# One-hots by source in fp8, and block sums of masks and hops added by VectorE

## The chip, the cores and the metric

The kernel runs on one core of a Trainium2 chip. The metric is the device time of one execution in microseconds. TensorE (PE) multiplies matrices into PSUM, VectorE (DVE) and ScalarE (ACT) do elementwise work, GpSimd (POOL) issues the indirect DMAs, SyncE (SP) issues the plain ones.

## The reference

Four layers of a graph network run on 6250 nodes with 64 features and 200000 edges (`src`, `dst`, 32 edge features): a gated convolution with batch norm, a mean aggregation, three masked hops, and a message MLP. The change touches the first layer's preparation and the three hops. One hop is:

```
f1 = relu(x[src] @ nb_W + nb_b);  f2 = relu(x[dst] @ self_W + self_b)
h = relu(concat(f1, f2) @ att1_W + att1_b)
mask = clip(sigmoid(h @ att2_W + att2_b) * 1.5 - 0.45, 0, 1)
rowsum = segment_sum(mask, src) + 1e-6
d = clip(rowsum ** -0.5, 0, 10)
x = segment_sum((mask * d[src] * d[dst])[:, None] * x[dst], src);  out = out + x
```

## The kernel before, in words

Nodes lie in 49 blocks of 128 (node on the partition). Edges are sorted by source and, separately, by destination into 288 batches (`NBT`, `IT`) of 7 chunks (`BATCH`, `C`) of 128 edges; all edges of a batch belong to one block, and a table of block numbers (`m.table_s` by source, `m.table_d` by destination) lies in SBUF. A segment sum over a batch is 7 times a matmul of a 128x128 one-hot matrix (edge by node in the block) with the edges' values. For fp32 accuracy a value is split into three bf16 parts, so it takes 3 matmuls a chunk.

Stages run one after another, with barriers between them. Inside a stage each engine has its own instruction list, a loop over the iterations (`each12` unrolls twelve, `each4` four), and semaphores order the engines. The order inside each list is written by hand. Stages that the change touches:

- `stage_conv_spread` (L1099, once): per iteration it loads 126 KB of records, compares (VectorE, L1176) the record's node number with 0..127 into the one-hot by source, stores it to DRAM as `hot_s` (L1138, 224 KB in bf16), transposes it on TensorE (L1253) into `turned_s` (fp8, 112 KB), transposes the edge features into `e_turned` (L1141, 224 KB), multiplies, and scatters 452 KB of rows. ScalarE copies out of PSUM (L1213, L1219, L1220, L1231).
- `stage_masks` (L1895, three times): TensorE multiplies `turned_s` with the block's row part (L2014), ScalarE lays that down in one of 12 column buffers (L1968), a GpSimd indirect DMA adds the gathered column part to it (L1956), VectorE makes the logit (L2047, L2052), and for each four iterations (a quad) ScalarE takes the sigmoid (L1973) and VectorE's `weigh` (L2030) makes the masks and their three parts. TensorE's `collect` (L1995) sums a quad's masks, three quads later, into `sums`, one PSUM bank that holds 3 numbers for each of the 49 blocks. The block number comes from a register (`Blocks.of`, L119, reads four numbers of the table at once, L121). Zero matmuls (`add_zeros`) open and close the bank; at the end one copy moves it to `rowsum` (L2058).
- `stage_hop` (L2061, three times): GpSimd gathers 224 KB of rows (L2104), ScalarE weighs six chunks (L2120) and VectorE the seventh (L2134), VectorE takes off the upper bf16 parts (L2143, L2149), and TensorE multiplies with the one-hots (L2167) into `sums`, 49 blocks of 64 numbers over seven PSUM banks, at the block of a register. The end is again zero matmuls and one copy (L2153).
- The conv messages stage is not changed, but has the other form already: its `collect` on VectorE (L1608) adds a fixed PSUM place to a block of `acc` (L1615).

One-hots by source are loaded in `stage_masks` by quads (896 KB) and in `stage_hop` by iterations (224 KB), both on SyncE's queue, twelve iterations ahead. One-hots by destination (`hot_d`) stay in bf16.

Of the kernel before, what the change touches and what calls it, by code (L numbers as in the profile page):

```python
# [13 lines left out]
P = 128  # L14
# [1084 lines left out]
def stage_conv_spread(nc, m, src3):  # L1099
# [5 lines left out]
    with ctx:  # L1105
# [10 lines left out]
        onehot = sb("onehot", [P, 4, BATCH, P], bf16)  # L1116
# [13 lines left out]
        with nc.Block() as block:  # L1130
# [35 lines left out]
            def _(dve):  # L1166
# [4 lines left out]
                def prepare(it, i, k):  # L1171
                    dve.wait_ge(came[i], k * 16 + 16)
                    dve.wait_ge(hot_stored[i], k * 16 + 16)
                    dve.wait_ge(turn, it + 1)
                    dve.sem_inc(gate, 1)
                    nc.vector.tensor_tensor(onehot[:, i, :, :], b2(m.iota_p[:], BATCH), b3(rec[:, i, :, EF], P),  # L1176
                                            ALU.is_equal).then_inc(hot, 1)
                    e = rec[:, i, :, 0:EF]
                    rest, last = e4[:, i % 2, :, 1, :], e4[:, i % 2, :, 2, :]
                    nc.vector.tensor_tensor(rest, e, upper(e), ALU.subtract).then_inc(order, 1)  # L1180
                    dve.wait_ge(order, it + 1)
                    dve.sem_inc(gate, 1)
                    nc.vector.tensor_tensor(last, rest, upper(rest), ALU.subtract).then_inc(parted, 1)
# [711 lines left out]
def stage_masks(nc, m, l, row_part3, mask, rowsum):  # L1895
# [5 lines left out]
    with ctx:  # L1901
# [6 lines left out]
        onehot = sb("onehot", [P, 3, 4, BATCH, P], bf16)  # L1908
# [10 lines left out]
        sums = ctx.enter_context(nc.psum_tensor(f"{name}_sums_ps", [P, 512], fp32))[:, 0:3 * NB].rearrange("p (b c) -> p b c", c=3)  # L1919
# [5 lines left out]
        with nc.Block() as block:  # L1925
# [64 lines left out]
            @block.tensor  # L1990
            def _(pe):
                quads = Blocks(nc, pe, m.table_s)
                add_zeros(nc, m, sums, True)

                def collect(quad, s, k):  # L1995
                    pe.wait_ge(hot_came[s], k * 16 + 16)
                    pe.wait_ge(masked, quad + 1)
                    pe.sem_inc(gate, 1)
                    for h in range(4):
                        blocks = quads.of(quad * 4 + h, h)  # L2000
                        for t in range(BATCH):
                            last = nc.tensor.matmul(block_of(sums, blocks[0]), onehot[:, s, h, t, :], mask3[:, s, h * BATCH + t, :],  # L2002
                                                    start=False, stop=False)
                    last.then_inc(summed, 1)

                def step(it, s, i, k, more, _):
                    pe.wait_ge(staged, it + 1)
                    if i == 0:
                        pe.wait_ge(came[s], k * 16 + 16)
                    pe.wait_ge(laid, it + 1)  # L2010
                    pe.sem_inc(gate, 1)
                    for t in range(BATCH):
                        for n in range(3):
                            last = nc.tensor.matmul(part_ps[i][:, t, :], turned[:, s, i, t, :], now[:, i, n, :],  # L2014
                                                    start=n == 0, stop=n == 2)
                    last.then_inc(part, 1)
                    if i == 3 and (not isinstance(it, int) or it > 11):
                        collect(k * 3 + s - 3, s, k - 1)
                each12(pe, step, first=12)
                for s in range(3):  # L2020
                    collect(QUADS - 3 + s, s, KQ - 1)
                add_zeros(nc, m, sums, False).then_inc(summed, 1)

            @block.vector
            def _(dve):
                o = Order(dve, order)
                dve.sem_inc(hid, 12)
                dve.sem_inc(logits, 2)

# [12 lines left out]
                def step(it, s, i, k, more, order):  # L2042
# [10 lines left out]
                    if i == 3 and (not isinstance(it, int) or it > 3):  # L2053
                        weigh(k * 3 + s - 1, (s - 1) % 3, k, order)
                each12(dve, step, first=16, o=o, per=3 * 5)
                weigh(QUADS - 1, 2, KQ - 1, o)
                dve.wait_ge(summed, QUADS + 1)
                nc.vector.tensor_copy(rowsum, sums)  # L2058


def stage_hop(nc, m, name, mask, acc):  # L2061
# [4 lines left out]
    with ctx:  # L2066
# [5 lines left out]
        onehot = sb("onehot", [P, 3, 4, BATCH, P], bf16)  # L2072
# [3 lines left out]
        sums = ctx.enter_context(nc.psum_tensor(f"{name}_sums_ps", [P, 56, F], fp32))  # L2076
# [4 lines left out]
        with nc.Block() as block:  # L2081
# [47 lines left out]
            def _(dve):  # L2129
# [8 lines left out]
                def step(it, s, i, k, more, _):  # L2138
# [10 lines left out]
                    nc.vector.tensor_tensor(last, rest, upper(rest), ALU.subtract).then_inc(parted, 1)  # L2149
                scale_seventh(0, 0, 0)  # L2150
                each12(dve, step)
                dve.wait_ge(summed, IT + 5)
                nc.vector.tensor_copy(acc, sums[:, 0:NB, :])  # L2153

            @block.tensor
            def _(pe):
                blocks_s = Blocks(nc, pe, m.table_s)
                add_zeros(nc, m, sums[:], True)

                def step(it, s, i, k, more, _):  # L2160
                    pe.wait_ge(came[s * 4 + i], k * 16 + 16)
                    pe.wait_ge(parted, it + 1)
                    blocks = blocks_s.of(it, i)
                    pe.sem_inc(gate, 1)
                    for t in range(BATCH):
                        for q in range(3):
                            last = nc.tensor.matmul(block_of(sums, blocks[0]), onehot[:, s, i, t, :],  # L2167
                                                    upper(parts[:, i, q, t * F:(t + 1) * F]), start=False, stop=False)
                    last.then_inc(summed, 1)
                each12(pe, step)  # L2170
                add_zeros(nc, m, sums[:], False).then_inc(summed, 1)


def build(nc, a, out):
    m = Net()
    top = ExitStack()
    with top:
# [24 lines left out]
        m.hot_s, m.hot_d = (dram(n, [P, NBT, C * P // 2]) for n in ("hot_s", "hot_d"))  # L2202
# [215 lines left out]
```

## Time and profile before

| | |
|---|---|
| median of 3 runs | 12580.16 us (12571.6 to 12588.71) |
| profiled execution | 12564.72 us, span 12563.0 us |
| conv spread stage | 2459 to 3425 us of the span |
| masks stages | from 6870, 8550 and 10231 us, about 598 us each |
| hop stages | from 7757, 9438 and 11117 us, about 457 us each |
| busy share | PE 63%, PEld 59%, DVE 65%, ACT 55%, POOL 41% |
| DMA | 3241.49 MB, mean 258 GB/s |

Busy time is the time in which an engine executes operations; register, branch and semaphore instructions are not in it. PE is the matmuls, PEld the weight loads beside them. In a group's row the part behind the bar is how long the engine stood idle just before these operations, and what ended most of that. `DVEq` and the like are an engine's sequencer. A window's row gives the busy times in the order PE, PEld, DVE, ACT, POOL. Start times count from the span's start.

### The profile page before, as it was taken

To read this page: it belongs to the slowest core of one execution; us is meant where nothing else is said; L and a number is where in the kernel's file an instruction comes from. 1 tells how busy PE (TensorE), PEld (TensorE's weight loads), DVE (VectorE), ACT (ScalarE), POOL (GpSimd) and SP (SyncE) were. 2 spreads that over 40 slices of the span, in tenths; PEclk is the share of its full clock that TensorE was granted. 3 is DMA by queue.
4 is the path that set the end of the run, shared out by engine and by line. 5 is a ranking of instruction groups with operands and counts; after the bars stand their busy time and mean duration, and the time that the engine had idled before them with its cause. 6 is when DMAs were issued, how large, how long until landed. Compare 5 with 4: busy or idle time off the path is not lost. (4 is left out here: it accounts for less than half of the span.)

```text
span 12563.0 us, 438885 instructions
## 1 busy us (share of the span) xinstructions
PE 7912.2 (63%) x149095; PEld 7405.0 (59%) x149106; DVE 8207.7 (65%) x17786; ACT 6913.4 (55%) x17614; POOL 5175.5 (41%) x4482
## 2 busy tenths in 40 slices
PE   6444444488855549995766656666666666565765
PEld 6333333488745448885656656565665566565765
DVE  6777777588799999981750762925718527358047
ACT  1222222299855559986217448965479764587530
POOL 2777777444300001110630752706707338345044
PEclk8555555599978879998979669787697787787997
DMA  5555543299967759987949999979999799997997
GB/s 205 166 171 167 169 140 84 83 348 348 326 195 202 201 173 319 323 275 264 346 127 349 288 262 354 297 263 300 284 324 316 226 329 290 290 335 231 366 361 226
DMA packets 1430365, 3241.49 MB, mean 258 GB/s; under 512 B 392074, under 2 KB 973252, under 8 KB 1419042
## 3 DMA queue, kind: packets, MB, share of 16 engines
q1 hardware_dynamic: 1054798, 2289.98, 52.1%
q0 software_dynamic: 331264, 823.09, 24.7%
q10 hardware_dynamic: 44116, 125.96, 3.3%
q8 instruction: 113, 1.85, 0.1%
q14 instruction: 74, 0.61, 0.0%
HBM read 2042.53 MB, written 1129.76 MB: 253 GB/s over the span
## 5 line engine op out<-in xcount | busy, mean ns | idle before, releaser
L1956 POOL DMA_INDIRECT mask_cols<-cols_all,mask_index x864 | 1372.1, 1588 | 1339.1 <-ACT mask_index L1965 1172.0
L521 POOL DMA_INDIRECT rows_s<-place_rec,place_index x1568 | 1631.1, 1040 | 538.1 <-issue 528.7
L596 PE MATMUL place_slot_ps<-place_runs,place_oh_turned 50*128 50x100 f32 x3136 | 725.8, 423 | 1231.6 <-DVE place_runs L635 1213.6
L2104 POOL DMA_INDIRECT hop_x<-cols_all,hop_index x864 | 981.2, 1136 | 1237.4 <-ACT hop_index L2111 920.0
L596 PEld LDWEIGHTS place_slot_ps<-place_runs,place_oh_turned 50*128 50x128 f32 x3136 | 683.0, 327 | 1265.9 <-issue 1265.6
L2120 ACT ACTIVATE hop_parts<-hop_x,mask 128x64 f32<-128x64 f32 x5184 | 1265.4, 334 | 47.6 <-DMA hop_x<-cols_all,hop_index 28.1
L2047 DVE SCALAR_TENSOR_TENSOR mask_hidden<-mask_cols,att 128x448 f32<-128x448 f32 x864 | 538.5, 623 | 1085.5 <-DMA mask_cols<-cols_all,mask_index 1028.8
L2167 PE MATMUL hop_sums_ps<-hop_parts,hop_onehot 128*128 128x64 bf16 x18144 | 876.0, 216 | 472.3 <-DVE hop_parts L2149 398.2
L2167 PEld LDWEIGHTS hop_sums_ps<-hop_parts,hop_onehot 128*128 128x128 bf16 x18144 | 777.0, 113 | 573.6 <-issue 572.7
L1478 POOL DMA_DIRECT2D cm_onehot<-hot_d x288 | 152.1, 528 | 2031.1 <-POOLq L104 1229.9
L2014 PE MATMUL mask_part_ps<-mask_now,mask_turned 128*128 128x64 bf16 x18144 | 912.5, 231 | 37.4 <-issue 20.9
L1968 ACT COPY mask_cols<-mask_part_ps 128x448 f32<-128x448 f32 x864 | 460.5, 533 | 841.2 <-PE mask_part_ps L2014 829.9
L550 ACT COPY place_pair_now<-place_pair 128x8 f32 x196 | 38.7, 197 | 1599.0 <-issue 1585.6
L2014 PEld LDWEIGHTS mask_part_ps<-mask_now,mask_turned 128*128 128x128 fp8e4 x18144 | 888.9, 124 | 42.9 <-issue 42.7
L2134 DVE TENSOR_TENSOR hop_parts<-hop_x,mask 128x64 f32<-128x64 f32 x864 | 189.6, 219 | 863.7 <-DMA hop_x<-cols_all,hop_index 845.0
L1687 PE MATMUL hop_in_rows_ps<-hop_in_now,hop_in_turned 128*128 128x64 bf16 x18144 | 571.7, 194 | 279.9 <-DMA hop_in_turned<-turned_d 134.0
L1687 PE MATMUL att_in_rows_ps<-att_in_now,att_in_turned 128*128 128x64 bf16 x18144 | 574.0, 194 | 253.3 <-DMA att_in_turned<-turned_d 115.6
L1687 PEld LDWEIGHTS hop_in_rows_ps<-hop_in_now,hop_in_turned 128*128 128x128 fp8e4 x18144 | 552.5, 99 | 299.4 <-issue 299.3
L1687 PEld LDWEIGHTS att_in_rows_ps<-att_in_now,att_in_turned 128*128 128x128 fp8e4 x18144 | 555.1, 99 | 272.5 <-issue 272.5
L1159 POOL DMA_INDIRECT rows_all<-cs_u,cs_index x288 | 393.9, 1368 | 639.1 <-DVE cs_u L1196 637.8
L2052 DVE TENSOR_REDUCE mask_logit<-mask_hidden 128x7 f32<-128x448 f32 x864 | 536.1, 621 | 131.2 <-DVE mask_hidden L2047 11.7
L2002 PE MATMUL mask_sums_ps<-mask_mask,mask_onehot 128*128 128x3 bf16 x6048 | 192.2, 166 | 669.5 <-DVE mask_mask L809 358.6
(392 smaller groups left out, 26453.3 us busy)
## 6 DMA issues: line engine op xcount, KB each, us to landing
cols_all<-att_in_rows SPq DMA_DIRECT2D x216, 896.0 KB
mask_onehot<-hot_s SPq DMA_DIRECT2D x216, 896.0 KB
cols_all<-hop_in_rows SPq DMA_DIRECT2D x216, 896.0 KB
hop_onehot<-hot_s SPq DMA_DIRECT2D x864, 224.0 KB
rows_all<-blank SPq DMA_DIRECT2D x72, 1808.0 KB
ct_u<-rows_all SPq DMA_DIRECT2D x288, 452.0 KB
cm_v<-rows_all SPq DMA_DIRECT2D x288, 448.0 KB
cm_onehot<-hot_d POOLq DMA_DIRECT2D x288, 448.0 KB
```

What stands on the lines that cost most here:

```text
L521: nc.gpsimd.indirect_dma_start(m.rows_s.rearrange("p n w -> (p n) w"), bass.IndirectOffsetOnAxis(index[:, j, t:t + 1], 0), rec[:, j, t, :] ...
L596: last = nc.tensor.matmul(slot_ps[b][:, t, 0:2 * NBK], oh_turned[:, b, t, :], runs[:, b, t, :], start=True, stop=True)
L1159: nc.gpsimd.indirect_dma_start(rows_d, bass.IndirectOffsetOnAxis(index[:, i, :], 0), u[:, i, :], None).then_inc(scattered[i], 16)
L1687: last = nc.tensor.matmul(rows_ps[i][:, t, :], turned[:, s, i, t, :], now[:, i, n, :], start=n == 0, stop=n == 2)
L1956: nc.gpsimd.indirect_dma_start(cols[:, n, :], None, table, bass.IndirectOffsetOnAxis(index[:, n, :], 0), compute_op=ALU.add).then_inc(arri ...
L1968: nc.scalar.copy(cols[:, n, :], part_ps[n % 4].rearrange("p c f -> p (c f)")).then_inc(laid, 1)
L2014: last = nc.tensor.matmul(part_ps[i][:, t, :], turned[:, s, i, t, :], now[:, i, n, :], start=n == 0, stop=n == 2)
L2047: nc.vector.scalar_tensor_tensor(out=hidden[:, j, :, :], in0=cols[:, s * 4 + i, :].rearrange("p (c f) -> p c f", f=F), scalar=0.0, in1=b2( ...
L2052: nc.vector.tensor_reduce(logit[:, s, i * BATCH:(i + 1) * BATCH], hidden[:, j, :, :], AX.X, ALU.add).then_inc(logits, 1)
L2104: nc.gpsimd.indirect_dma_start(x[:, n, :, :].rearrange("p c f -> p (c f)"), None, table, bass.IndirectOffsetOnAxis(index[:, n:n + 1], 0)). ...
L2120: last = nc.scalar.activation(parts[:, i, 0, t * F:(t + 1) * F], x[:, s * 4 + i, t, :], ACT.Copy, scale=mask[:, bass.ds(it * BATCH + t, 1)])
L2167: last = nc.tensor.matmul(block_of(sums, blocks[0]), onehot[:, s, i, t, :], upper(parts[:, i, q, t * F:(t + 1) * F]), start=False, stop=False)
```

## The change

One-hots by source are made, stored and loaded in fp8 instead of bf16; 0 and 1 are exact in both. In `stage_masks` and `stage_hop` TensorE no longer accumulates all iterations into a table of blocks in PSUM. Each iteration's sum goes to a fixed place (in masks one bank for each of three quads in flight, with four places in it; in the hop one of four banks), opened and closed by the iteration's own first and last matmul. VectorE then adds that place to the block of `rowsum` or of `acc` in SBUF, at the block number that it now reads from the table itself, and counts its adds in a new semaphore `added`, for which TensorE waits before it uses the place again. In masks the adds of quad q - 4 come at the end of quad q, behind `weigh` of quad q - 1; in the hop those of iteration it - 2 behind L2149. `rowsum` and `acc` are set to zero at the start. The zero matmuls and the final copies go.

```diff
# stage_conv_spread
-        onehot = sb("onehot", [P, 4, BATCH, P], bf16)
+        onehot = sb("onehot", [P, 4, BATCH, P], fp8)
...
-                                            ALU.is_equal).then_inc(hot, 1)
+                                            ALU.is_equal, saturate=False).then_inc(hot, 1)
 # stage_masks
-        onehot = sb("onehot", [P, 3, 4, BATCH, P], bf16)
+        onehot = sb("onehot", [P, 3, 4, BATCH, P], fp8)
...
-        sums = ctx.enter_context(nc.psum_tensor(f"{name}_sums_ps", [P, 512], fp32))[:, 0:3 * NB].rearrange("p (b c) -> p b c", c=3)
+        sums = [ctx.enter_context(nc.psum_tensor(f"{name}_sums_ps{j}", [P, 512], fp32))[:, 0:12].rearrange("p (h c) -> p h c", c=3)
+                for j in range(3)]
...
-                quads = Blocks(nc, pe, m.table_s)
-                add_zeros(nc, m, sums, True)
-
                 def collect(quad, s, k):
                     pe.wait_ge(hot_came[s], k * 16 + 16)
                     pe.wait_ge(masked, quad + 1)
+                    pe.wait_ge(added, quad * 4 + 4)
                     pe.sem_inc(gate, 1)
                     for h in range(4):
-                        blocks = quads.of(quad * 4 + h, h)
                         for t in range(BATCH):
-                            last = nc.tensor.matmul(block_of(sums, blocks[0]), onehot[:, s, h, t, :], mask3[:, s, h * BATCH + t, :],
-                                                    start=False, stop=False)
+                            last = nc.tensor.matmul(sums[s][:, h, :], onehot[:, s, h, t, :], mask3[:, s, h * BATCH + t, :],
+                                                    start=t == 0, stop=t == BATCH - 1)
...
-                add_zeros(nc, m, sums, False).then_inc(summed, 1)
...
+                dve.sem_inc(added, 11)
+                quads = Blocks(nc, dve, m.table_s)
+                nc.vector.memset(rowsum, 0.0).then_inc(added, 1)
+
+                def add_rows(quad, s):
+                    dve.wait_ge(summed, quad + 1)
+                    for h in range(4):
+                        blocks = quads.of(quad * 4 + h, h)
+                        dve.wait_ge(added, quad * 4 + 12 + h)
+                        dve.sem_inc(gate, 1)
+                        to = block_of(rowsum, blocks[0])
+                        nc.vector.tensor_tensor(to, to, sums[s][:, h, :], ALU.add).then_inc(added, 1)
...
                     if i == 3 and (not isinstance(it, int) or it > 3):
                         weigh(k * 3 + s - 1, (s - 1) % 3, k, order)
+                    if i == 3 and (not isinstance(it, int) or it > 18):
+                        add_rows(k * 3 + s - 4, (s - 1) % 3)
...
-                dve.wait_ge(summed, QUADS + 1)
-                nc.vector.tensor_copy(rowsum, sums)
+                for quad in range(QUADS - 4, QUADS):
+                    add_rows(quad, quad % 3)
 # stage_hop
-        onehot = sb("onehot", [P, 3, 4, BATCH, P], bf16)
+        onehot = sb("onehot", [P, 3, 4, BATCH, P], fp8)
...
-        sums = ctx.enter_context(nc.psum_tensor(f"{name}_sums_ps", [P, 56, F], fp32))
+        sums = [ctx.enter_context(nc.psum_tensor(f"{name}_sums_ps{j}", [P, 512], fp32))[:, 0:F] for j in range(4)]
...
+                    if not isinstance(it, int) or it > 1:
+                        collect(it - 2, (i - 2) % 4)
+
+                def collect(it, i):
+                    blocks = table_s.of(it, i)
+                    dve.wait_ge(summed, it + 5)
+                    dve.wait_ge(added, it + 4)
+                    dve.sem_inc(gate, 1)
+                    to = block_of(acc, blocks[0])
+                    nc.vector.tensor_tensor(to, to, sums[i], ALU.add).then_inc(added, 1)
+                table_s = Blocks(nc, dve, m.table_s)
+                dve.sem_inc(added, 3)
+                nc.vector.memset(acc, 0.0).then_inc(added, 1)
...
-                dve.wait_ge(summed, IT + 5)
-                nc.vector.tensor_copy(acc, sums[:, 0:NB, :])
+                collect(IT - 2, (IT - 2) % 4)
+                collect(IT - 1, (IT - 1) % 4)
...
                     pe.wait_ge(parted, it + 1)
-                    blocks = blocks_s.of(it, i)
+                    pe.wait_ge(added, it + 1)
...
-                            last = nc.tensor.matmul(block_of(sums, blocks[0]), onehot[:, s, i, t, :],
-                                                    upper(parts[:, i, q, t * F:(t + 1) * F]), start=False, stop=False)
+                            last = nc.tensor.matmul(sums[i], onehot[:, s, i, t, :],
+                                                    upper(parts[:, i, q, t * F:(t + 1) * F]),
+                                                    start=t == 0 and q == 0, stop=t == BATCH - 1 and q == 2)
 # build
-        m.hot_s, m.hot_d = (dram(n, [P, NBT, C * P // 2]) for n in ("hot_s", "hot_d"))
+        m.hot_s, m.hot_d = dram("hot_s", [P, NBT, C * P // 4]), dram("hot_d", [P, NBT, C * P // 2])
```

## Rows read from the trace of the kernel before

**Rows 1.** The first line of the page

```profile
span 12563.0 us, 438885 instructions
```

**Rows 2.** Windows: length, busy us (operations) by engine, clock, DMA share, GB/s

```profile
2459.00:3425.00 966.00, 831.61 (x14028) 790.21 (x14028) 802.17 (x2287) 867.85 (x1433) 391.04 (x285) 0.99 0.98 344
6870.00:7468.00 598.00, 366.35 (x8065) 355.59 (x8065) 442.32 (x1081) 274.00 (x938) 456.33 (x288) 0.67 1.06 277
7770.00:8120.00 350.00, 235.86 (x5051) 208.38 (x5049) 333.37 (x723) 350.00 (x1503) 275.60 (x240) 0.80 0.94 315
8120.00:8205.00 85.00, 48.41 (x907) 42.87 (x905) 61.12 (x133) 65.98 (x270) 42.68 (x39) 0.62 0.96 211
```

**Rows 3.** The DMA view of 2500 to 3400, inside the conv spread stage

```profile
DMA packets 175949, 312.88 MB, mean 348 GB/s; under 512 B 21455, under 2 KB 158744, under 8 KB 175949
```

**Rows 4.** Groups in 6870 to 7468: busy us, mean ns | idle before

```profile
L1956 POOL DMA_INDIRECT mask_cols<-cols_all,mask_index x288 | 456.3, 1584 | 444.9 <-ACT mask_index L1965 391.2 <-issue 46.6 <-ACT mask_cols L1968 7.0
...
L2047 DVE SCALAR_TENSOR_TENSOR mask_hidden<-mask_cols,att 128x448 f32<-128x448 f32 x288 | 179.4, 623 | 360.4 <-DMA mask_cols<-cols_all,mask_index 341.6 <-issue 11.0 <-DVE mask_logit L2052 4.1
```

**Rows 5.** Timeline of GpSimd in a masks stage: start us, length us

```profile
7299.42 1.54 POOL L1956 DMA_INDIRECT mask_cols<-cols_all,mask_index  x1 [0.30 <-issue]
7301.27 1.54 POOL L1956 DMA_INDIRECT mask_cols<-cols_all,mask_index  x1 [0.30 <-issue]
```

**Rows 6.** Timeline of VectorE in the first masks stage

```profile
6922.05 0.61 DVE L2047 SCALAR_TENSOR_TENSOR mask_hidden<-mask_cols,att 128x448 f32<-128x448 f32 x1
6922.81 0.62 DVE L2052 TENSOR_REDUCE mask_logit<-mask_hidden 128x7 f32<-128x448 f32 x1
6923.35 0.17 DVE L2037 TENSOR_SCALAR mask_mask_now<-mask_logit 128x28 f32<-128x28 f32 x1
6923.55 0.18 DVE L2038 TENSOR_SCALAR mask_mask_now<-mask_mask_now 128x28 f32<-128x28 f32 x1
6923.90 0.18 DVE L2039 COPY mask<-mask_mask_now 128x28 f32 x1 [0.17 <-DVE mask_mask_now L2038]
...
6924.93 0.63 DVE L2047 SCALAR_TENSOR_TENSOR mask_hidden<-mask_cols,att 128x448 f32<-128x448 f32 x1
```

**Rows 7.** Timeline at the start of the first masks stage

```profile
6869.67 1.52 SPq L1929 DMA_DIRECT2D mask_turned<-turned_s  x3
...
6885.20 0.62 DVE L2047 SCALAR_TENSOR_TENSOR mask_hidden<-mask_cols,att 128x448 f32<-128x448 f32 x1 [287.57 <-DMA mask_cols<-cols_all,mask_index]
```

**Rows 8.** Timeline of VectorE in the first hop stage

```profile
8001.19 0.63 DVE L2143 TENSOR_TENSOR hop_parts<-hop_parts 128x448 f32<-128x448 f32 x1
8001.73 0.22 DVE L2134 TENSOR_TENSOR hop_parts<-hop_x,mask 128x64 f32<-128x64 f32 x1
8001.97 0.62 DVE L2149 TENSOR_TENSOR hop_parts<-hop_parts 128x448 f32<-128x448 f32 x1
8002.63 0.62 DVE L2143 TENSOR_TENSOR hop_parts<-hop_parts 128x448 f32<-128x448 f32 x1
```

**Rows 9.** Groups in 2459 to 3425, ScalarE and TensorE

```profile
L1213 ACT COPY cs_e<-cs_rec 128x448 f32<-128x448 f32 x288 | 162.7, 565 | 73.7 <-PE cs_e_ps L1255 37.8 <-DMA cs_rec<-rows_s 30.3
...
L1253 PE MATMUL cs_turn_ps<-ident_b,cs_onehot 128*128 128x128 bf16 x2009 | 158.8, 219 | 141.3 <-ACT cs_e_turned L1220 131.3 <-DVE cs_e L1183 9.4 <-issue 0.6
```

**Rows 10.** The DMA view of 7490 to 7750, a plain spread stage

```profile
DMA packets 20078, 96.37 MB, mean 371 GB/s; under 512 B 2223, under 2 KB 2223, under 8 KB 20074
```

**Rows 11.** Groups in 7768 to 8214, the first hop stage

```profile
L2167 PE MATMUL hop_sums_ps<-hop_parts,hop_onehot 128*128 128x64 bf16 x6048 | 289.0, 215 | 159.7 <-DVE hop_parts L2149 135.5 <-DMA hop_onehot<-hot_s 15.5 <-issue 4.2
...
L2153 DVE COPY H<-hop_sums_ps 128x3136 f32<-128x3136 f32 x1 | 3.4, 3424 | 2.6 <-PE hop_sums_ps L132 2.6
```

**Rows 12.** Line L121, the table read, VectorE's sequencer (min/median/max ns)

```profile
L121 DVEq TENSOR_LOAD <-table_d x72: 340/344/607, 4708.3 to 5619.6; - x72
```

**Rows 13.** Timeline of VectorE in the conv messages stage

```profile
5001.38 0.39 DVE L1615 TENSOR_TENSOR acc<-acc,cm_sums_ps 128x64 f32 x1
5001.51 1.26 DVE L1591 TENSOR_TENSOR cm_v<-cm_v_ps,cm_v 128x896 f32<-128x896 f32 x1
```

More of the change, by code:

```diff
@@ L1918, in stage_masks @@
         part_ps = [ctx.enter_context(nc.psum_tensor(f"{name}_part_ps{j}", [P, 8, F], fp32))[:, 0:BATCH, :] for j in range(4)]
-        sums = ctx.enter_context(nc.psum_tensor(f"{name}_sums_ps", [P, 512], fp32))[:, 0:3 * NB].rearrange("p (b c) -> p b c", c=3)
+        sums = [ctx.enter_context(nc.psum_tensor(f"{name}_sums_ps{j}", [P, 512], fp32))[:, 0:12].rearrange("p (h c) -> p h c", c=3)
+                for j in range(3)]
+        added = sem("added")
         came, hot_came = [sem(f"came{s}") for s in range(3)], [sem(f"hot_came{s}") for s in range(3)]
@@ L2075, in stage_hop @@
         parts = sb("parts", [P, 4, 3, BATCH * F])
-        sums = ctx.enter_context(nc.psum_tensor(f"{name}_sums_ps", [P, 56, F], fp32))
+        sums = [ctx.enter_context(nc.psum_tensor(f"{name}_sums_ps{j}", [P, 512], fp32))[:, 0:F] for j in range(4)]
+        added = sem("added")
         came, arrived = [sem(f"came{n}") for n in range(12)], [sem(f"arrived{n}") for n in range(12)]
@@ L2149, in step @@
                     nc.vector.tensor_tensor(last, rest, upper(rest), ALU.subtract).then_inc(parted, 1)
+                    if not isinstance(it, int) or it > 1:
[10 more added lines that the diff above has]
+                nc.vector.memset(acc, 0.0).then_inc(added, 1)
                 scale_seventh(0, 0, 0)
-                each12(dve, step)
-                dve.wait_ge(summed, IT + 5)
-                nc.vector.tensor_copy(acc, sums[:, 0:NB, :])
+                each12(dve, step, first=2)
+                collect(IT - 2, (IT - 2) % 4)
+                collect(IT - 1, (IT - 1) % 4)
             @block.tensor
             def _(pe):
-                blocks_s = Blocks(nc, pe, m.table_s)
-                add_zeros(nc, m, sums[:], True)
                 def step(it, s, i, k, more, _):
@@ L2166, in step @@
                         for q in range(3):
-                            last = nc.tensor.matmul(block_of(sums, blocks[0]), onehot[:, s, i, t, :],
-                                                    upper(parts[:, i, q, t * F:(t + 1) * F]), start=False, stop=False)
+                            last = nc.tensor.matmul(sums[i], onehot[:, s, i, t, :],
+                                                    upper(parts[:, i, q, t * F:(t + 1) * F]),
+                                                    start=t == 0 and q == 0, stop=t == BATCH - 1 and q == 2)
                     last.then_inc(summed, 1)
                 each12(pe, step)
-                add_zeros(nc, m, sums[:], False).then_inc(summed, 1)
 def build(nc, a, out):
```

## The prediction

> **What bounds the kernel now.** The page's first line [rows 1] gives 12563.0 us of span; the profiled execution took 12564.72 us in all, 15.4 under the median of 12580.16. My sum starts from 12564.72, and 15.4 is added at its end. The stages have different limits, so I read one window per stage that the change touches [rows 2], then the groups inside each, and last VectorE's instructions in order.
>
> The conv spread stage (2459 to 3425) does 288 iterations in 966 us, 3.36 each. DMA share is 0.98, ScalarE is busy 867.85 us (3.01 per iteration), TensorE 831.61 (2.89), VectorE 802.17 (2.79) [rows 2]. In its middle the rate is 348 GB/s [rows 3], 1.167 MB per iteration. The transfers set the pace, with ScalarE close behind.
>
> The masks stage (three times, the first from 6870 to 7468) takes 598 us. VectorE is busy 442.32 us [rows 2] and stands before L2047 for gathered rows [rows 4]; part of those 341.6 us lies ahead of the stage. A gather costs GpSimd 1584 ns in the mean [rows 4] and 0.30 us between two of them (1.54 us long, 1.85 apart [rows 5]), so 1.88 us, 7.5 for four. VectorE's own need, read where it doesn't wait [rows 6]: 1.30 us per iteration (6922.05 to 6923.35), and 1.58 for the seven small operations of `weigh` (6923.35 to 6924.93). A group of four iterations needs 4 x 1.30 + 1.58 = 6.78 us. It takes 8.09: from the first L2047 at 6885.20 [rows 7] to 7468 are 582.8 us for 72 groups. VectorE has 1.3 us to spare in each.
>
> The hop stage (three times) has two parts. In the first 350 us VectorE runs 723 operations, three per iteration: 241 iterations of 1.45 us, ScalarE busy 350.00 of 350, VectorE 333.37, 95% [rows 2]. In the next 85 us it runs 133, 44 iterations of 1.93, at 211 GB/s against 315: slower gathers. VectorE's order in the first part is L2143, L2134 0.54 later, L2149 0.23 later, L2143 again 0.66 later [rows 8]: 1.43.
>
> **Part 1: fp8 one-hots in the spread stage.** The comparison still writes 896 elements from fp32 operands; I price the narrower output at nothing, and VectorE's 0.57 us of slack per iteration (3.36 - 2.79) hides it if it costs more. The store falls from 224 to 112 KB, 0.115 MB less: 1.052 MB, 3.02 us at 348 GB/s. ScalarE needs 3.01 and still waits 30.3 us for records and 37.8 for TensorE before L1213, and TensorE stands 131.3 us before L1253 until ScalarE's copy is done [rows 9]: a ring whose floor is a little over 3.01. I take 3.10: (3.36 - 3.10) x 288 = -75 us. Bounds: -98 by the bytes alone, 0 if that ring holds the pace; likely -95 to -35.
>
> The packets that halve go from 1792 to 896 bytes. Where they are 1.8 KB on average (312.88 MB in 175949) the rate is 348 GB/s [rows 3], where they are 4.8 KB it is 371 [rows 10]: size counts little. The Trainium skill, "Perfetto Trace Analysis", DMA Optimizations, says that transfers under 2 KB have significant per-transfer overhead. Taken to its end, half a packet costs as much as a whole one, and part 1 would be 0, not -75; that is my third rival.
>
> **Part 2: loads of one-hots in masks and hop.** They halve too (896 to 448 KB per four iterations, 224 to 112 KB per iteration). In masks VectorE waits for the gathers, which GpSimd issues at its own pace. In hop TensorE waits 15.5 us per stage for one-hots [rows 11], beside the slow gathers. I take 0, with -15 per hop as the bound; the DMA share of 1.06 in masks makes a gain there my first rival.
>
> **Part 3: what leaves TensorE.** The table reads, the address arithmetic and the zero matmuls go; matmuls keep number and shape. TensorE is busy 366 of 598 us in masks [rows 2] and stands 135.5 us before L2167 for VectorE in hop [rows 11], so none of this is on the path, but for the hop's end: the copy of H, 3.42 us, and the 2.6 us that it waited for the last matmuls [rows 11] go, and two small adds come. -5 per hop. The memset of H lies where VectorE waits for the first gather.
>
> **Part 4: VectorE's adds in masks.** In each group of four, behind `weigh`, come one read of the block table into registers and four adds of 128x3 from PSUM, each at a register's address, each waiting for the one before it. The trace has no such add; nearest are `weigh`'s operations of 128x28, 0.17 to 0.18 us [rows 6]. A dependent follower starts 0.20 us later when its address is fixed (6923.35 to 6923.55), 0.35 when a register gives it (6923.55 to 6923.90). An add also waits through a counted semaphore with a gate of its own, as L2052 does, 0.77 behind a 0.62 operation (6922.05 to 6922.81), 0.15 from end to start. With 0.18 for itself, 0.17 for the address and 0.10 for the wait I take 0.45 per add. Ahead of the first stand the table read, 0.344 us on the sequencer [rows 12], a threshold, two waits and the address, 0.7 us in all; behind the last, the next step's threshold and wait, 0.25. Sum 0.7 + 3 x 0.45 + 0.25 = 2.3 us per group. Bounds: 4 x 0.20 + 0.40 = 1.2, when waits and registers don't show; 4 x 0.60 + 0.7 = 3.1. By the nearest rows 1.9 to 2.9.
>
> VectorE then needs 6.78 + 2.3 = 9.08 us per group, over GpSimd's 7.5 and today's 8.09: it is the bound. Queued behind the adds on VectorE is the next L2047, which frees column buffers for the gathers. TensorE's `collect` gets a wait for adds that stand just behind the `weigh` it waits for already; before VectorE needs the rows that depend on it, two groups pass, 18 us, and the whole start of a stage, with loads, takes 15.5 us [rows 7], so I charge nothing. One stage: 15.5 to the first L2047, 72 x 9.08 = 654, some 3 for its end, 673 instead of 598: +75 x 3 = +225.
>
> **Part 5: VectorE's adds in the hop.** Each iteration gets one add of 128x64 from PSUM behind L2149, of the kind of L1615 in the conv messages stage, where the next operation starts 0.13 us behind it (5001.38 to 5001.51 [rows 13]). The engine's floor is 0.54 + 0.23 + 0.54 + 0.13 = 1.44, level with ScalarE. To that comes the sequencer's work from L2149 to the next L2143 (thresholds, waits, address), about 0.7 us against 0.66 now, and in every fourth iteration the table read [rows 12] with its register work, +0.5 in the open. (3 x 1.47 + 1.95) / 4 = 1.59, with the loop's branch 1.60, against 1.45: +0.15 x 241 = +35 per stage. The last part's 1.93 hides it. With the -5 of part 3: +30 x 3 = +90. Bounds per iteration 0 (ScalarE hides it) and +0.42 (0.22 for the add, 0.20 for register work, all in the open): -15 to +290 for three stages.
>
> **Sum.** 12564.7 - 75 + 225 + 90 = 12804.7, + 15.4 = 12820 us, +1.9%.
>
> **Rivals.** First, faster: the transfers set the masks, and VectorE's idle time swallows the adds. For it: share 1.06, 1.3 us to spare, half the one-hot bytes gone. Against it: 2.3 is more than 1.3. It decides below 1.3 us per group. At 0.7 the pace is GpSimd's 1.88: 288 x 1.88 + 18.5 = 560, -38 x 3 = -114, with -75 and -15: 12376. A weaker form, 1.3 per group and a hop left as it is, gives 12580 - 75 - 15 = 12490. Chance 9%.
>
> Second, dearer adds: register work begins only when the engine has drained. Masks at 2.9 per group: 72 x 9.68 + 18.5 = 715, +117 x 3 = +351; hop +0.35 per iteration: (84 - 5) x 3 = +237. With -75: 13093. For it: the idle time at a register's address in [rows 6]. Against it: in [rows 13] the add is followed at once. Chance 15%.
>
> Third, half the bytes buy nothing in the spread stage: 12820 + 75 = 12895. For it: ScalarE at 3.01 and its ring. Against it: 348 GB/s in the stage's mean, near the 371 of a stage that only moves data. Chance 14%.
>
> My forecast keeps 62%.
>
> **How the numbers follow.** The likeliest is 12820. Likely ends of the parts: masks +130 to +350, hop -15 to +240, spread -95 to -35. They don't all fall to one side, so 12650 to 13060 holds about 8 in 10; it leaves out the faster rival and the top of the second. The likeliest case alone spans 12720 to 12920. A measurement tells 0.2%, 25 us, from no change. Faster: the first rival and a little of the low end, 10%; within: 4%; slower: 86%.
>
> **What the profile after would show.** Spread: the rate near 348 GB/s and 3.1 us per iteration; at 3.3 the third rival has it. Masks: little wait before L2047, 9 us per group, adds 0.45 apart; at 0.25 apart the first rival. Hop: ScalarE idle for the first time, VectorE at 1.6 with one long iteration in four. A masks stage under 598 us, or the hop's first 241 iterations under 350, would make the prediction wrong.

## The result, and the profile after

The changed kernel takes 12796.06 us (median of 4 runs, 12784.75 to 12806.58); the kernel before takes 12584.43 in the runs beside it. The ratio is 1.0169, with an interval of 1.0154 to 1.0184. The prediction was 12820.

Lengths of masks and hops below run from the stage's first instruction to the next stage's first, those of the spread from ScalarE's first copy in it to VectorE's last, each read from one profiled execution per kernel. (Expectations written before a run read a hop from VectorE's first product in it, 5 to 7 us later, and masks 1 us shorter.) The total is the median of the runs, or the one time where there was a single run. In the runs masks_rotated, spread_unrolled, combined, after_again and combined_again, which the table leaves out, every kernel, the one before too, took 6 to 7% longer (hops of 527 to 539 us, spreads of 978 to 987, masks as elsewhere), so each is read against its neighbours.

| kernel | spread | masks, three | hop, three | total us |
|---|---|---|---|---|
| before | 974.9 | 598.4, 601.0, 598.6 | 457.7, 457.8, 459.7 | 12584.43 |
| after | 933.0 | 675.1, 678.6, 682.7 | 468.4, 468.4, 470.2 | 12796.06 |
| bf16_adds | 975.1 | 678.7, 684.0, 685.8 | 476.7, 476.0, 479.2 | 12859.76 |
| fixed_blocks | 933.2 | 613.8, 612.2, 611.7 | 447.5, 447.5, 446.5 | 12528.86 |
| spread_no_store | 919.7 | 674.5, 678.3, 682.1 | 466.5, 465.9, 468.1 | 12770.58 |
| spread_two_stores | 1005.6 | 673.6, 678.6, 681.6 | 464.3, 465.3, 467.8 | 12855.64 |
| combined_third | 933.0 | 615.3, 608.8, 616.2 | 469.0, 468.0, 468.8 | 12588.78 |
| reads_hidden | 934.5 | 586.3, 580.7, 579.6 | 453.4, 453.5, 453.7 | 12464.45 |

After minus before is -42 in the spread, +238 in the masks and +32 in the hops: +228 together, and the spans differ by 228.4. So nothing moved outside these seven stages. The page's first line and the windows of the four stretches that answer to [rows 1, 2] (length, busy us of PE, PEld, DVE, ACT, POOL, clock, DMA share, GB/s):

```profile
span 12791.4 us, 443643 instructions
...
2459.00:3392.00 933.00, 836.64 (x14112) 794.91 (x14112) 786.90 (x2304) 865.15 (x1440) 308.78 (x287) 0.99 0.94 323
6832.00:7505.00 673.00, 366.24 (x8064) 357.15 (x8064) 478.08 (x1368) 269.02 (x938) 450.06 (x288) 0.66 0.93 197
7770.00:8140.00 370.00, 257.00 (x5003) 231.00 (x5000) 325.40 (x877) 343.96 (x1423) 231.94 (x227) 0.67 0.80 231
8145.00:8225.00 80.00, 51.79 (x979) 46.27 (x976) 71.47 (x193) 71.60 (x296) 48.96 (x48) 0.65 0.90 184
```

In the masks stage GpSimd's and TensorE's busy time is as before, VectorE's rose by only 36 us, and the stage by 77. The other half is idle time of VectorE between its own instructions, which a busy share doesn't show. In the hop's first part TensorE's granted clock is 0.67, where it was 0.80; VectorE's plain iterations take 1.43 to 1.44 us at either (see below), so this costs nothing that the rows show. The groups of that stage (busy us, mean ns, then idle before and its enders), answering to [rows 4]:

```profile
L1958 POOL DMA_INDIRECT mask_cols<-cols_all,mask_index x288 | 450.1, 1563 | 523.2 <-ACT mask_index L1967 462.6 <-issue 46.0 <-ACT mask_cols L1970 14.6
...
L2057 DVE SCALAR_TENSOR_TENSOR mask_hidden<-mask_cols,att 128x448 f32<-128x448 f32 x288 | 177.9, 618 | 37.0 <-DMA mask_cols<-cols_all,mask_index 19.0 <-issue 16.2
...
L2001 PE MATMUL mask_sums_ps<-mask_mask,mask_onehot 128*128 128x3 bf16 x2016 | 63.5, 166 | 295.5 <-DVE rowsum L2038 277.2 <-DVE mask_mask L809 18.4
...
L2038 DVE TENSOR_TENSOR rowsum<-rowsum,mask_sums_ps 128x3 f32 x288 | 45.4, 158 | 95.6 <-DVE rowsum L2038 53.3 <-issue 42.3
```

VectorE's wait for gathered rows is 19.0 us, 13 of them at the start of the stage. Of the 341.6 us before, 272 lie ahead of the stage (287.57 less the 15.5 from the stage's start to the first L2047, [rows 7]), so inside the stage it fell from about 70. VectorE is the bound now. The adds are busy 45.4 us and stand idle 95.6: two thirds of their price is waiting. `collect` on TensorE now waits 277.2 us for adds; nothing needs its result sooner, so this wait costs nothing. VectorE's order (start us, length us), answering to [rows 6]:

```profile
7048.23 0.21 DVE L809 TENSOR_TENSOR mask_mask<-mask_mask_now,mask_mask 128x28 bf16<-128x28 f32 x1
7049.05 0.16 DVE L2038 TENSOR_TENSOR rowsum<-rowsum,mask_sums_ps 128x3 f32 x1 [0.62 <-issue]
7049.46 0.16 DVE L2038 TENSOR_TENSOR rowsum<-rowsum,mask_sums_ps 128x3 f32 x1 [0.25 <-DVE rowsum L2038]
7049.86 0.16 DVE L2038 TENSOR_TENSOR rowsum<-rowsum,mask_sums_ps 128x3 f32 x1 [0.24 <-DVE rowsum L2038]
7050.26 0.16 DVE L2038 TENSOR_TENSOR rowsum<-rowsum,mask_sums_ps 128x3 f32 x1 [0.24 <-DVE rowsum L2038]
7050.49 0.62 DVE L2057 SCALAR_TENSOR_TENSOR mask_hidden<-mask_cols,att 128x448 f32<-128x448 f32 x1
```

The add takes 0.16 us, and the next starts 0.40 behind it. From L809 to the first add are 0.82 us, with the table read among them; to the next L2057 are 2.26, where in the kernel before 0.22 stood between L809 and the L2047 of 6924.93 in [rows 6]:

```profile
6924.71 0.21 DVE L809 TENSOR_TENSOR mask_mask<-mask_mask_now,mask_mask 128x28 bf16<-128x28 f32 x1
```

In the hop (answering to [rows 8]), two adds in a row and, further on, one behind a table read:

```profile
7832.78 0.21 DVE L2172 TENSOR_TENSOR H<-H,hop_sums_ps 128x64 f32 x1
7832.91 0.62 DVE L2156 TENSOR_TENSOR hop_parts<-hop_parts 128x448 f32<-128x448 f32 x1
7833.45 0.22 DVE L2147 TENSOR_TENSOR hop_parts<-hop_x,mask 128x64 f32<-128x64 f32 x1
7833.68 0.64 DVE L2162 TENSOR_TENSOR hop_parts<-hop_parts 128x448 f32<-128x448 f32 x1
7834.24 0.21 DVE L2172 TENSOR_TENSOR H<-H,hop_sums_ps 128x64 f32 x1
...
7835.13 0.63 DVE L2162 TENSOR_TENSOR hop_parts<-hop_parts 128x448 f32<-128x448 f32 x1
7835.94 0.22 DVE L2172 TENSOR_TENSOR H<-H,hop_sums_ps 128x64 f32 x1 [0.17 <-PE hop_sums_ps L2190]
```

From L2162 to its add are 0.54 to 0.56 us as a rule (7833.68 to 7834.24) and 0.81 behind a read (7835.13 to 7835.94). The row puts the 0.17 in front of that add down to TensorE, but the sequencer's wait for the sum lasts 0.05 us there; what lies in front of it is the table read, 0.34. Iterations take 1.44 us, and 1.74 to 1.78 in four of twelve: three reads, and one jump of the twelve-fold loop. Mean 1.55.

The spread stage, its DMA view (answering to [rows 3]) and its groups (to [rows 9]):

```profile
DMA packets 173657, 278.04 MB, mean 327 GB/s; under 512 B 21185, under 2 KB 156746, under 8 KB 173657
```

```profile
L1176 DVE TENSOR_TENSOR cs_onehot<-iota_p,cs_rec 128x896 fp8e4<-128x896 f32 x288 | 312.1, 1084 | 11.6 <-DMA cs_rec<-rows_s 5.8 <-issue 0.3 <-PE cs_e_ps L1255 0.3
...
L1213 ACT COPY cs_e<-cs_rec 128x448 f32<-128x448 f32 x288 | 163.8, 569 | 6.9 <-DMA cs_rec<-rows_s 6.4 <-PE cs_e_ps L1255 0.4
...
L1253 PE MATMUL cs_turn_ps<-ident_b,cs_onehot 128*128 128x128 bf16 x2016 | 159.3, 219 | 102.9 <-ACT cs_e_turned L1220 67.8 <-DVE cs_e L1183 23.4 <-issue 11.7
...
L1192 DVE COPY cs_u<-cs_rec 128x7 f32<-128x7 f32 x288 | 49.2, 171 | 93.0 <-PE cs_u_ps L1271 90.1
```

The rate fell from 348 to 327 GB/s and the share from 0.98 to 0.94: the transfers no longer set the pace. ScalarE doesn't wait for records any more (30.3 to 6.4 us), but VectorE waits for TensorE and TensorE for ScalarE: 3.22 us per iteration, of which ScalarE is busy 3.01.

### The profile page after: what moved, and what is told of

It reads as the page before. It is cut to its first block and busy times, and to the rows that moved or that the text cites. A ratio compares the mean times of both kernels' runs of the same rounds, so it can differ in the third digit from the quotient of the medians.

```text
span 12791.4 us, 443643 instructions
## 1 busy us (share of the span) xinstructions
PE 8002.8 (63%) x149053; PEld 7508.7 (59%) x149058; DVE 8371.7 (65%) x19514; ACT 6917.9 (54%) x17614; POOL 4988.1 (39%) x4482
## 5 line engine op out<-in xcount | busy, mean ns | idle before, releaser
L2117 POOL DMA_INDIRECT hop_x<-cols_all,hop_index x864 | 891.0, 1031 | 1403.2 <-ACT hop_index L2124 942.2
L2190 PE MATMUL hop_sums_ps<-hop_parts,hop_onehot 128*128 128x64 bf16 x18144 | 972.9, 225 | 445.7 <-DVE H L2172 266.7
L2190 PEld LDWEIGHTS hop_sums_ps<-hop_parts,hop_onehot 128*128 128x128 fp8e4 x18144 | 872.9, 119 | 545.7 <-issue 545.6
L2001 PEld LDWEIGHTS mask_sums_ps<-mask_mask,mask_onehot 128*128 128x128 fp8e4 x6048 | 178.7, 103 | 919.2 <-issue 919.2
L2057 DVE SCALAR_TENSOR_TENSOR mask_hidden<-mask_cols,att 128x448 f32<-128x448 f32 x864 | 533.7, 618 | 111.7 <-DMA mask_cols<-cols_all,mask_index 57.9
L1271 PE MATMUL cs_u_ps<-cs_now,cs_turned 128*128 128x128 bf16 x6048 | 578.8, 219 | 0.0
```

Source lines behind the costliest of these rows:

```text
L1271: last = nc.tensor.matmul(at, turned[:, i, t, :], now[:, i, n, :], start=False, stop=n == 2)
L2057: nc.vector.scalar_tensor_tensor(out=hidden[:, j, :, :], in0=cols[:, s * 4 + i, :].rearrange("p (c f) -> p c f", f=F), scalar=0.0, in1=b2( ...
L2117: nc.gpsimd.indirect_dma_start(x[:, n, :, :].rearrange("p c f -> p (c f)"), None, table, bass.IndirectOffsetOnAxis(index[:, n:n + 1], 0)). ...
L2190: last = nc.tensor.matmul(sums[i], onehot[:, s, i, t, :], upper(parts[:, i, q, t * F:(t + 1) * F]), start=t == 0 and q == 0, stop=t == BAT ...
```

## The experiments

**bf16_adds**: the adds alone, one-hots in bf16 everywhere.

```diff
-        onehot = sb("onehot", [P, 4, BATCH, P], fp8)
+        onehot = sb("onehot", [P, 4, BATCH, P], bf16)
... (the same in stage_masks, stage_hop and for hot_s)
```

> The adds of masks and hop as in the changed kernel, but the one-hots by source stay in bf16 (made, stored and loaded as before). Theory A (the adds on VectorE are the whole loss, the narrower transfers only help the conv spread stage and the slow last part of the hop): conv spread 966 us as before, masks +75 to +80 each (673 to 680), hop +17 each instead of +13, so 12584 + 235 + 50 = about 12870. Theory B (the half-size loads hide part of the cost in masks too): masks over +90 each, total over 12910.

Measured 12859.76 us, ratio 1.0234 (1.0217 to 1.0251) to the kernel before at 12561.35. The spread is back at 975.1. The fp8 one-hots are thus worth about 0.65%, some 80 us: 42 in the spread, 3 to 5 in each masks stage, 8 to 9 in each hop. Those small gains in masks and hop weren't in the sum. The losses, 80 to 87 us per masks stage and 18 to 20 per hop here, belong to the other half of the change, the adds: theory A, with masks a little dearer than it said.

**fixed_blocks**: VectorE adds each place to a fixed block. It leaves out the table reads and the register addresses.

```diff
-                        blocks = quads.of(quad * 4 + h, h)
...
-                        to = block_of(rowsum, blocks[0])
+                        to = rowsum[:, h, :]
... (in the hop: to = acc[:, i, :], without table_s.of)
```

> The changed kernel with the block number left out: VectorE adds each place to a block fixed in the program, so the table read and the address arithmetic are gone, the waits stay. Block sums therefore land in the wrong blocks. Theory A (table read 0.45 us and about 0.10 us of address per add stand in the open): masks group from 9.11 to about 8.25 us, stage about 611; hop from 1.549 to 1.46 us per iteration, stage 20 us less. Theory B (the wait of each add for the one before is the cost, registers are hidden): group 8.7 or more, hop hardly changed.

Measured 12528.86 us. VectorE in a masks stage, and the window of that stage:

```profile
7053.48 0.21 DVE L809 TENSOR_TENSOR mask_mask<-mask_mask_now,mask_mask 128x28 bf16<-128x28 f32 x1
7053.71 1.07 DVE L2037 TENSOR_TENSOR rowsum<-rowsum,mask_sums_ps 128x3 f32<-128x3 f32 x4
```

```profile
6875.00:7470.00 595.00, 347.09 (x7550) 338.38 (x7551) 469.85 (x1351) 259.75 (x886) 424.05 (x271) 0.65 0.96 209
```

The first add starts 0.23 us behind L809 (0.82 with the read and the address), four take 1.07, about 0.30 apart, where only the wait for the one before is left. The stages take 612 to 614 us, where the change takes 675 to 683: theory A. A hop falls by 21 to 24, to 10 to 13 under the kernel before: its first 241 iterations take 1.46 to 1.47 us, as before (1.46), so the adds themselves are free there, and register work is the whole loss and more.

**spread_no_store** and **spread_two_stores**: the store of the one-hots left out (masks and hops then read `turned_s` in their place), and the fp8 store made twice, to another tensor.

```diff
-                    sp.dma_start(m.hot_s[:, bass.ds(it, 1), :], as_words(onehot[:, i, :, :])).then_inc(hot_stored[i], 16)
+                    sp.sem_inc(hot_stored[i], 16)
```

```diff
+                    sp.dma_start(m.hot_again[:, bass.ds(it, 1), :], as_words(onehot[:, i, :, :])).then_inc(hot_stored[i], 16)
```

> The changed kernel without the store of the one-hots by source in the conv spread stage; masks and hops load the transposed ones in their place, of the same size, so their sums are of other edges. Theory A (the stage at 3.22 us per iteration is now set by the ring of ScalarE, TensorE and VectorE with the loop's jump, not by transfers): 3.18 to 3.22 us, stage 920 to 933. Theory B (transfers still set it): 0.94 MB at 327 GB/s is 2.87, so ScalarE's 3.01 to 3.05 holds, stage about 880.

> The changed kernel with the fp8 one-hots by source stored twice, to two tensors, in rows of 896 bytes: the bytes of the bf16 kernel in twice as many packets for this store. Theory A (bytes count, packets of 896 bytes cost in proportion): 3.35 to 3.38 us per iteration as before, stage about 968. Theory B (a packet costs nearly the same at 896 as at 1792 bytes): about 3.6 us, stage over 1010. Theory C (transfers do not bind at all, before neither): 3.22, stage 933.

The DMA views of 2500 to 3350, first without the store, then with two:

```profile
DMA packets 137485, 251.20 MB, mean 296 GB/s; under 512 B 17179, under 2 KB 120333, under 8 KB 137485
```

```profile
DMA packets 195850, 285.47 MB, mean 336 GB/s; under 512 B 23506, under 2 KB 180171, under 8 KB 195850
```

Without the store the stage takes 919.7 us, 13 under the change, at 296 GB/s and a share of 0.83: theory A, the engines' ring holds it at 3.18 per iteration. Leaving out this store wholly gives no more than that. Of the store's whole weight the change took 42 of 55 us. With two stores, the bytes of bf16 in packets of half the size, it takes 1005.6, 31 more than with one bf16 store, at 3.48 us per iteration: between theory A's 3.38 and theory B's 3.6. ScalarE's first copy waits for records again, in the group of that stretch:

```profile
L1214 ACT COPY cs_e<-cs_rec 128x448 f32<-128x448 f32 x246 | 139.2, 566 | 102.5 <-DMA cs_rec<-rows_s 72.5 <-PE cs_e_ps L1256 29.6
```

A packet itself costs in proportion to its size (43 ns at 896 bytes, 88 at 1792). The records' own packets, of 1008 bytes, take 47 ns in the mean in the kernel before, 61 in the change, 64 without the store and 57 here, so they don't follow the count of packets. Whether the number of packets, their semaphore writes or the second issue on SyncE's queue costs the 31 us stays open.

**masks_rotated**: four copies of the row sums, one per place, so that an add waits for the last group's only.

```diff
+                    dve.wait_ge(added, quad * 4 + 12)
+                    dve.sem_inc(gate, 1)
                     for h in range(4):
...
-                        dve.wait_ge(added, quad * 4 + 12 + h)
-                        dve.sem_inc(gate, 1)
-                        to = block_of(rowsum, blocks[0])
+                        to = block_of(rows4[:, h, :, :], blocks[0])
```

> The changed kernel, but in masks the four adds of a quad go to four tables (one per place in the quad) that one reduction sums at the stage's end; one wait stands before the four adds, none between them. Theory A (each add's start is held by its wait for the one before: 0.396 us apart): now about 0.15 apart, a group of four iterations 9.11 - 0.72 = 8.4 us, stage about 622. Theory B (the register's address and the PSUM read hold them): 0.25 to 0.35 apart, stage 640 or more.

Measured 13520.52 us beside 13471.88 for the kernel before. The masks take 622.9, 623.2 and 624.2 us instead of 675 to 683, theory A. VectorE's timeline:

```profile
7470.55 0.58 DVE L2040 TENSOR_TENSOR mask_rows<-mask_rows,mask_sums_ps 128x3 f32 x4 [0.92 <-issue]
7471.21 0.62 DVE L2059 SCALAR_TENSOR_TENSOR mask_hidden<-mask_cols,att 128x448 f32<-128x448 f32 x1
```

Four adds in 0.58 us, 0.14 apart, at register addresses: the address costs nothing when the sequencer can run ahead. It costs when a wait for the engine's own last result stands between two of them. What is left is the time before the first.

**spread_unrolled**: the spread's loops unrolled by twelve.

```diff
-                each4(act, step, first=4)
+                each4_by12(act, step, first=4)
... (on every engine)
```

> The changed kernel with the loop of the conv spread stage unrolled twelve times instead of four. Theory A (of the four phases of 3.09, 3.49, 3.05 and 3.21 us the long one is the loop's jump in the engines' ring): two of three jumps go, about 3.14 us per iteration, stage about 912. Theory B (the long one is the read of the block table, which stays at every fourth iteration): 3.2, stage 930.

The spread takes 987.3 us, and 984.1 in masks_rotated beside it, which isn't unrolled; combined_third, unrolled too, takes the 933.0 of the change. The loop's jump isn't what makes 3.22 out of 3.18; that theory falls. The rhythm of ScalarE's L1219 in the change (3.09, 3.49, 3.04, 3.21, repeating by four) becomes 3.09, 3.30, 3.04, 3.21 without the store: the 13 us of transfers are all in the long one. That it stays the longest fits the table read of every fourth iteration, but no run took that read away.

**combined**, **combined_again**, **combined_third**: rotated sums, spread unrolled, and one read of twelve block numbers for each twelve iterations in masks and hop; the same kernel three times.

```diff
+            self.table[0:1, bass.ds(it, self.n)], engines=[self.eng.engine], min_val=0, max_val=NB - 1,
...
+                    if n == 0:
+                        table_s.read(it)
```

> The changed kernel with three edits together: the spread loop unrolled twelve times, masks with four tables and one wait, and in masks and hop the block numbers read by VectorE twelve at a time instead of four. If theory A holds throughout: spread about 912 us, masks group 8.1 us and stage about 600, hop 1.47 us per iteration and stage about 445; together 12584 - 62 + 9 - 24, about 12510, ratio 0.994 to the kernel before. If the adds stay dear (theory B): masks over 625, total about 12600, ratio 1.00 or more.

> The changed kernel once more, beside the combined one, so that their stages stand side by side under one condition. Both theories: the stages as in its first profile, spread 933, masks 674 to 681, hop 463 to 465 us.

> The combined kernel once more. Its first executions, and those of the kernel before beside them, were all 7% longer (13472 and 13472 us), with hop stages of 530 us in which VectorE and ScalarE wait for TensorE and for semaphores, so the hop's part could not be read. Theory A: masks about 606 us, hop about 445, spread about 912; 12510 to 12540 where the kernel before takes 12580, ratio 0.994 to 0.997. Theory B (the hop's adds cost the same however the table is read, and the spread loop gains nothing): hop 463, spread 933, masks 606 to 610, ratio 1.000 or a little above.

> The kernel before, for its stages beside those of the combined kernel under the same condition. If the executions are 7% longer again, both theories expect its hop stages near 520 us too, since the extra time would be in the transfers and not in the adds; if they are back at 12560 to 12590, spread 966, masks 598 and hop 451 as in the first profile.

> The combined kernel a third time. If executions are back at 12580: theory A says masks 608, hop 445, spread 933, about 12545, ratio 0.996 to 0.998; theory B says hop 463, ratio 1.000 to 1.002. If they are 7% longer again: ratio 1.000 as twice before.

Ratios to the kernel before: 0.9999 (0.999 to 1.0008), 0.9999 (0.999 to 1.0008) and 1.0003 (0.9993 to 1.0012), at 13472.44, 13327.53 and 12588.78 us. The changed kernel beside the second took 13549.64 to 13331.05, the 1.016 of its first run. The kernel before, profiled once more, took 12585.59, its stages up to 6 us longer than in its first profile: so much two profiles of one kernel differ. The masks fell to 609 to 616; the hop gained nothing, 468 to 469 (first 241 iterations 370.0 us instead of 373.7, the rest 88.0 instead of 82.7). The two forms of the table read on VectorE's sequencer (ns, min/median/max), of the change and of combined_third:

```profile
L121 DVEq TENSOR_LOAD <-table_s x432: 339/344/1031, 6883.6 to 11797.5; - x144
```

```profile
L134 DVEq TENSOR_LOAD <-table_s x144: 846/857/1699, 6890.4 to 11586.4; - x144
```

Twelve numbers at once take 857 ns, four 344. One iteration of 2.26 to 2.31 us in twelve stands in place of three of 1.76: a bigger read mostly gathers the cost in one place. Theory B holds: only the rotated sums gained.

**reads_hidden**: rotated sums, the spread as in the change; in masks the group's read goes between the logit's product and its reduction; in the hop one number is read in every iteration between `scale_seventh` and the wait for `halved`, where the sequencer waits for the engine anyway.

```diff
                         scale_seventh(it + 1, n % 12, k + n // 12)
+                    if not isinstance(it, int) or it > 1:
+                        read(it - 2)
                     dve.wait_ge(halved, it + 1)
...
+                    if i == 3 and (not isinstance(it, int) or it > 18):
+                        quads.of((k * 3 + s - 4) * 4, 0)
                     dve.wait_ge(hid, it + 13)
```

> The changed kernel with masks' four tables and one wait (as in the run with four tables), and with VectorE's reads of the block numbers moved to where its sequencer waits anyway: in masks behind the issue of the product of the fourth iteration, ahead of the wait for it; in the hop one number per iteration, ahead of the wait for L2156's kind of subtraction. The spread loop is as in the changed kernel. Theory A (a table read costs its 0.35 us only where nothing else is waited for): masks group 8.39 - 0.45, about 7.95, stage 585 to 600; hop 1.45 to 1.47 us per iteration, stage about 442; spread 933; total 12796 - 3 x 80 - 3 x 21 = about 12490, ratio 0.992. Theory B (a read holds the sequencer, and with it the issue of what follows, wherever it stands): masks 620, hop 463 or more, ratio over 1.000.

Measured 12464.45 us (12446.49 to 12476.28, 5 runs) beside 12558.86, ratio 0.9920 (0.9906 to 0.9933). It is faster than both kernels, theory A. VectorE in its masks, and then in its hop:

```profile
7105.32 0.21 DVE L809 TENSOR_TENSOR mask_mask<-mask_mask_now,mask_mask 128x28 bf16<-128x28 f32 x1
7105.64 0.58 DVE L2041 TENSOR_TENSOR mask_rows<-mask_rows,mask_sums_ps 128x3 f32 x4
7106.39 0.63 DVE L2060 SCALAR_TENSOR_TENSOR mask_hidden<-mask_cols,att 128x448 f32<-128x448 f32 x1 [0.18 <-issue]
```

```profile
7832.09 0.62 DVE L2171 TENSOR_TENSOR hop_parts<-hop_parts 128x448 f32<-128x448 f32 x1
7832.63 0.21 DVE L2185 TENSOR_TENSOR H<-H,hop_sums_ps 128x64 f32 x1
7832.76 0.62 DVE L2163 TENSOR_TENSOR hop_parts<-hop_parts 128x448 f32<-128x448 f32 x1
7833.29 0.22 DVE L2154 TENSOR_TENSOR hop_parts<-hop_x,mask 128x64 f32<-128x64 f32 x1
7833.52 0.62 DVE L2171 TENSOR_TENSOR hop_parts<-hop_parts 128x448 f32<-128x448 f32 x1
```

The part from L809 to the next L2060 is 1.07 us (7105.32 to 7106.39), against 2.26 in the change (7048.23 to 7050.49). Groups take 7.5 to 8.0 us as a rule, 7.8 to 7.9 in the mean. All hop iterations but the one at the loop's jump (2.02) are 1.44 to 1.50, mean 1.50 against 1.55. The stages give -51 in the masks, -15 in the hops and -40 in the spread against the kernel before, -106; the runs give -94. The masks are now 12 to 20 us under the kernel before, although VectorE does more in them. Whether the halved loads or the block reads gone from TensorE bring that, no run separates: none has hidden reads with bf16 one-hots.

## Why the prediction was right, step by step

The forecast's mechanism held: in the masks VectorE took over as the bound, and the adds' waits and registers were its price. Its sum gave +240 us for the seven stages, where +228 was measured: the spread came out 33 us worse, the masks 13 worse, the hops 58 better. So the closeness of the total is in part luck: errors cancelled, among the stages and inside the masks. The other 12 of the 24 us to the median are the 15.4 that I added for it; here the median is within 4 us of the profiled execution.

- **Spread, -75: measured -42.** This is the mis-sized term. The step "I take 3.10" put the ring's floor near ScalarE's 3.01 busy. The floor is 3.18 even with this store left out (spread_no_store). At 3.22 the change is near it. The rate, too, was to stay near 348 GB/s and fell to 327. The third rival (nothing gained) had the direction of the error right, not its reason: half the bytes did buy time, since with bf16 the stage is back at 975.1. The Trainium skill ("Perfetto Trace Analysis", DMA Optimizations) says that transfers under 2 KB carry a significant overhead each. Taken to its end, as in the third rival, that would have made it 0; the measured 42 us speaks against this, and the 31 us of the doubled store speak for some price.
- **Loads, 0: -8 to -9 per hop and -3 to -5 per masks stage** (bf16_adds against the change). The bound of -15 per hop covers the first.
- **What leaves TensorE, -5 per hop: -3 to -4.** From the last L2143 (now L2156) to the next stage are 8.2 to 8.4 us before and 3.9 to 5.1 after. With the halved loads it is what the hop has gained where adds cost nothing, 10 to 13 us in fixed_blocks.
- **Masks, +225: measured +238.** The group was to take 9.08 us and takes 9.07, 9.14 and 9.19 in the three stages. That is closer than the terms deserve. Inside it, 0.45 per add was 0.40; 0.7 ahead of the first is 0.82; 0.25 behind the last is 0.23 (7050.26 to 7050.49). Those make 2.25 from L809 to the next L2057. But the 6.78 to which I added them holds the 0.22 that stood between these two before (L809 at 6924.71, L2047 at 6924.93), so the adds cost 2.04 and not 2.3, and a plain group takes 6.78 + 2.04 = 8.82. What brings the mean back to 9.1 is the jump of the twelve-fold loop, where every third group is 9.56 instead of 8.82 to 9.0; I had no term for it. VectorE's wait before L2057 is 19.0 us, as foretold, and the wait of `collect` costs nothing. The end of the stage does cost: the sums of the last four quads are added there, and from the last group's first L2057 to the next stage are 17.9 us, where 11.6 were before; the start, with halved loads, gives 2 of them back (13.5 instead of 15.5).
- **Hop, +90: measured +32.** This is the other mis-sized term. The term per iteration, 1.60, was 1.55: without a read 1.44 and not 1.47, and a read adds 0.31, not 0.5. So the first 241 iterations lost 22 us and not 35 (351.9 to 373.7 in the first hop). The last part, which I left at 1.93, takes 1.80 with the halved loads, 6 us less, and the stage starts 1.8 us sooner. ScalarE idles as foretold, busy 343.96 of 370.
- **Rivals.** The first, transfers set the masks, would have needed adds of 1.3 us a group; they take 2.04, and the stage's DMA share is 0.93. The second, dearer adds, fell with 0.40 per add and a hop at 1.55. fixed_blocks and masks_rotated show what the price is made of: 0.10 of 0.40 is the address behind a wait, 0.16 the wait itself, 0.14 the add.

## What to carry to other kernels

Moving a small accumulation to another engine is priced by that engine's sequencer, not by the add: 0.14 us for the add, 0.40 with a wait for its own last result and a register address behind it, and 0.3 to 0.6 for a table read with its address in the open. Give consecutive adds different accumulators, and put a register read ahead of a wait that stands there anyway; here both together turned +1.7% into -0.8%, with the fp8 one-hots in either. Before counting on fewer bytes, find the pace of the stage without them: here the bytes promised 0.34 us per iteration and the ring of engines, at 3.18 us, let 0.15 of it through.

## What the runs showed of the hardware

- A table read into VectorE's registers takes 305 ns for one number (reads_hidden, in the hop), 344 for four and 857 for twelve (combined_third): three more cost 39 ns, eight more 513.
- VectorE compares 128x896 into fp8 in 1084 ns and into bf16 in 1092 (bf16_adds); TensorE loads these one-hots as 128x128 weights of either type in 97 ns in the spread stage. What the narrower type gained here came from the transfers alone.
- The same bytes in twice the packets made a stage at a DMA share of 0.97 longer by 31 us (1005.6 against 974.9), though a packet's own time halved, 88 to 43 ns.
- The jump of a twelve-fold loop shows on a VectorE without slack: +0.3 us in the changed hop, +0.6 to 0.7 in the masks.
